# A fused attention and feed-forward kernel on eight cores: one tile's norm per iteration, a pool of eighteen weight buffers, and later quantizing

## What is computed

```python
x = x + layernorm(linear_attn(layernorm(x), W_qkv, W_o))   # 16 heads of 64, chunks, causal, running state S
x = x + layernorm(ffn(layernorm(x)))
# ffn: h = layernorm(x) * gamma + beta
#      h = qlinear(h, w1, b1);  h = gelu(h);  out = qlinear(h, w2, b2)
# qlinear: activations to int8 range by row maximum;
#          weights to -1, 0, 1 by  scale = 1 / mean(|w|);  wq = clip(round(w * scale), -1, 1)
```

## Time and profile before

| what | value |
|---|---|
| median of 3 runs | 1594.47 us (1594.02 to 1597.79) |
| the profiled execution's own time | 1600.33 us |
| its span on the slowest core (core 3) | 1598.8 us |
| spans of the 8 cores | 1577.0 to 1598.8 us |
| PE busy | 1469.1 us, 92% of the span |
| DVE, ACT, POOL busy | 1116.4, 663.3, 277.9 us |

### The profile page before, as it was taken

One profiled execution on the slowest core, in us unless ns is written; L12 is line 12 of the kernel. 1 busy time (PEld: TensorE's weight loads), 2 busy tenths in 40 slices (PEclk: granted clock), 3 DMA queues, 4 the chain that ended last, 5 costly groups with the idle time before them and its releaser, 6 DMA issues.

```text
span 1598.8 us, 26641 instructions; the slowest of 8 cores (1577.0 to 1598.8 us)
## 1 busy us (share of the span) xinstructions
PE 1469.1 (92%) x8948; PEld 727.3 (45%) x8948; DVE 1116.4 (70%) x1861; ACT 663.3 (41%) x1057; POOL 277.9 (17%) x210
## 2 busy tenths in 40 slices
PE   1499589999999999699999999999999999999997
PEld 0255255655555555334444444444444444444443
DVE  6545257676887876677777767777676777767764
ACT  1088478676655555323223232232322323223231
POOL 2011124454676675000000000000000000000000
PEclk9799799999999999899999999999999999999999
DMA  9968957777889985333342533424244242342422
GB/s 226 261 190 241 176 157 217 198 228 219 191 196 200 207 194 160 90 91 78 83 99 61 111 70 81 100 61 114 67 88 94 60 113 69 93 88 60 104 51 66
DMA packets 284005, 209.94 MB, mean 131 GB/s; under 512 B 246616, under 2 KB 246616, under 8 KB 283872
## 3 DMA queue, kind: packets, MB, share of 16 engines
q1 hardware_dynamic: 261776, 131.16, 36.0%
q0 software_dynamic: 22096, 77.08, 17.9%
HBM read 119.03 MB, written 33.55 MB: 95 GB/s over the span
## 4 chain that ended last, share of the span: by engine, by line
PE 63%; DMA 15%; issue 8%; ACT 4%; DVE 3%; DVEq 3%; POOL 2%; ACTq 1%; SPq 0%; POOLq 0%
PE pz L437 28%; PE pp L425 27%; DMA pc<-w 10%; PE pp L315 3%; DMA wost<-w_o 2%; POOL lt L1099 2%; DMA h1f<-h1t 2%; ACT pc L887 1%; PE pp L416 1%; PE pp L333 1%; PE pp L401 1%; DMA kst<-w_qkv 1%; DVEq L723 1%; DVEq L510 1%; DVE wqtp L567 1%
## 5 line engine op out<-in xcount | busy, mean ns | idle before, releaser
L425 PE MATMUL pp<-w1p,xq1f 128*128 128x512 fp8e4 x2048 | 456.5, 381 | 0.0
L437 PE MATMUL pz<-w2p,xq2f 128*128 128x512 fp8e4 x2048 | 447.1, 379 | 0.0
L437 PEld LDWEIGHTS pz<-w2p,xq2f 128*128 128x128 bf16 x2048 | 200.4, 98 | 241.7
L425 PEld LDWEIGHTS pp<-w1p,xq1f 128*128 128x128 bf16 x2048 | 195.8, 98 | 243.5 <-issue 19.2
L636 DVE TENSOR_REDUCE st<-gsb 128x1 f32<-128x1024 f32 x128 | 152.6, 1213 | 130.5 <-ACT gsb L895 130.3
L901 ACT ACT_TABLE_LOAD x31 | 39.8, 1283 | 470.1 <-DVE st L675 470.1
L1099 POOL TENSOR_SCALAR lt<-pc,st 128x1024 bf16<-128x1024 f32 x64 | 188.9, 2952 | 144.5 <-DMA pc<-w 103.7
L895 ACT ACTIVATE gsb<-pp,st 128x1024 f32<-128x1024 f32 x128 | 142.3, 1112 | 102.6 <-PE pp L425 96.8
L315 PE MATMUL pp<-wk,h1f 128*128 128x512 bf16 x512 | 121.9, 391 | 39.2 <-DMA h1f<-h1t 32.4
L315 PE MATMUL pp<-wv,h1f 128*128 128x512 bf16 x512 | 129.7, 399 | 25.3 <-ACT kt L836 14.3
L333 PE MATMUL pp<-h1f,wq 128*128 128x256 bf16 x1024 | 122.6, 280 | 14.0 <-DMA h1f<-h1t 8.9
(11 more groups left out here) (111 smaller groups left out, 1392.2 us busy)
## 6 DMA issues: line engine op xcount, KB each, us to landing
pc<-w POOLq DMA_DIRECT2D x128, 512.0 KB, 6.1
xs<-x SPq DMA_DIRECT2D x32, 512.0 KB, 6.0
x1s<-xs SPq DMA_DIRECT2D x32, 512.0 KB, 4.4
xs<-x1s SPq DMA_DIRECT2D x32, 512.0 KB, 3.4
out<-xs SPq DMA_DIRECT2D x32, 512.0 KB, 3.1
kst<-w_qkv SPq DMA_DIRECT2D x8, 512.0 KB, 12.0
wost<-w_o POOLq DMA_DIRECT2D x8, 512.0 KB, 38.5
wq<-w_qkv POOLq DMA_DIRECT2D x1, 2048.0 KB, 21.4
```

The lines of the kernel that those rows point to most:

```text
L425: mi = PE.matmul(half(n, h), lhsT=xf[:, kk, :], rhs=w1q[:, kk % 4, c0:c0 + 512, kk // 4], start=False, stop=(kk == 7), skip_group_check=True)
L437: mi = PE.matmul(PZ[:, h * 512:(h + 1) * 512], lhsT=xq2f[:, t % 2, kk, :], rhs=w2q[:, kk % 16, h * 512:(h + 1) * 512, kk // 16], start=(kk ...
```

## The change

1. **Norm.** One tile per iteration, three ahead (f = i + 3), in place of two in each even iteration. On DVE `ln1(f)` stands first in the iteration, from i = -1 on. On ACT `ln1_sd(f)` stands right behind `ln2_sd` and `h1(f)` behind `ln3_sd`. On SP `h1_tp(f)` now stands behind the tile load and the first piece's transpose.
2. **Buffers.** All 18 piece buffers form one pool; each load takes the free buffer that was released longest ago, until w1p or w2p covers it. Two loads are in flight, not four. Seven pieces of w1 and five of w2 stay in their buffers from the sum to the quantizing, so that 116 loads remain of 128.
3. **Sums.** 23 of the 64 sums move from ACT to DVE (`piece_vsum`, a reduction of 128 x 1024 float32). Iteration 0 has none. ACT's sums in iterations 1 to 8 are 4, 5, 4, 1, 2, 2, 5, 4, DVE's 2, 1, 1, 5, 3, 4, 1, 1.
4. **Quantizing.** It now runs from iteration 9 to 31: up to 4 pieces in one, 2 in each of the last three. w2 is taken in order of its columns, 0 to 31. PE waits for w2p only ahead of the first `ffn2`.
5. **Layout.** w1p is stored as 32 blocks of 4 x 128, w2p as 8 blocks of 16 x 128, so that a piece's transpose writes one run. The right-hand operand of every `ffn1` and `ffn2` matmul is now four runs of 128 columns, where it was one of 512.
6. **Gamma and beta** are loaded by SP in iteration 30, no longer by POOL.

The diff, cut to its core:

```diff
-    w1p = at("w1p", O_W1, [4, HID], BF16)
+    w1p = at("w1p", O_W1, [NWP, 4, 128], BF16)
...
-    w2p = at("w2p", O_W2, [16, D], BF16)
+    w2p = at("w2p", O_W2, [8, 16, 128], BF16)
...
+    gap, hold = 12, (7, 5)
...
+    bufs = ([pc[:, k] for k in range(2)] + [pc1[:, k] for k in range(8)]
+            + [pc2[:, k] for k in range(8)])
+    covered = ([4 * NWP] * 2 + [place[("quant", 0, 4 * k)] for k in range(8)]
+               + [place[("quant", 1, 4 * k)] for k in range(8)])
+    held = [-1] * 10 + [8] * 8
...
+        z = min((b for b in own if end < covered[b]), key=lambda b: held[b])
...
-                                       rhs=w1q[:, kk % 4, c0:c0 + 512, kk // 4],
+                                       rhs=w1q[:, c0 // 128:c0 // 128 + 4, kk % 4, :, kk // 4],
...
-                                   rhs=w2q[:, kk % 16, h * 512:(h + 1) * 512, kk // 16],
+                                   rhs=w2q[:, 4 * h:4 * h + 4, kk % 16, :, kk // 16],
...
+        def piece_vsum(p):
+            buf, s_ld, landed = piece_buf(p)
+            V.wait_ge(s_ld, landed)
+            V.tensor_reduce(out=c1((acc1, acc2)[p[1]], p[2]), in_=buf, axis=AX.X, op=ALU.add,
+                            apply_absolute_value=True).then_inc(s_vabs, 1)
...
-            t, u, f = i, i + 1, i + 2
-            two = i % 2 == 0 and f < T
-            if two:
+            t, u, f = i, i + 1, i + 3
+            if f < T:
                 ln1(f)
             if 0 <= t - 1 < T:
                 x1(t - 1)
-            if two:
+            if f < T:
                 ln1_r(f)
...
+            if t == T - 2:
+                SP.wait_ge(s_Q, 2 * T)
+                SP.dma_start(out=gam[:], in_=gamma_h.partition_broadcast(128)
+                             ).then_inc(s_gbl[0], 16)
...
+        def load(n):
+            p = loads[n]
+            buf, s_ld, _ = piece_buf(p)
+            if n >= 2:
+                GP.wait_ge(piece_buf(loads[n - 2])[1], piece_buf(loads[n - 2])[2])
+            o, used = prior[p]
+            if not used and where[p][0] >= 10:
+                GP.wait_ge(s_oc, 8)
+            if used and pieces[o][0] == "quant":
+                GP.wait_ge(s_q, nqua[o] + 1)
+            if used and on_dve(pieces[o]):
+                GP.wait_ge(s_vabs, nvsum[o] + 1)
+            if used and pieces[o][0] == "sum" and not on_dve(pieces[o]):
+                GP.wait_ge(s_abs, nsum[o] + 1)
...
+        for q, p in enumerate(pieces):
+            while n < len(loads) and prior[loads[n]][0] <= q - 2:
+                load(n)
+                n += 1
+            if p[0] == "quant":
+                below(p)
```

More of the change, by code:

```diff
@@ new lines, in build @@
+    held = [-1] * 10 + [8] * 8
+    count = [0] * 18
+    loads, where, prior = [], {}, {}
+    for p in pieces:
+        if p[0] == "quant" and p[2] < hold[p[1]]:
+            where[p] = where[("sum", p[1], p[2])]
+            continue
+        stays = p[0] == "sum" and p[2] < hold[p[1]]
+        end = place[("quant", p[1], p[2])] if stays else place[p]
+        own = range(2 + 8 * p[1], 10 + 8 * p[1]) if stays else range(18)
+        z = min((b for b in own if end < covered[b]), key=lambda b: held[b])
+        count[z] += 1
+        where[p] = (z, 16 * count[z])
+        prior[p] = (held[z], count[z] > 1)
+        held[z] = end
+        loads.append(p)
@@ L286, in q_of, with piece_buf, sums_under @@
+    def piece_buf(p):
+        return bufs[where[p][0]], s_pl[where[p][0]], where[p][1]
+    def sums_under(k, z):
+        under = [place[p] for p in pieces
+                 if p[0] == "sum" and not on_dve(p) and where[p][0] == 2 + 8 * k + z // 4]
+        return nsum[max(under)] + 1 if under else 0
     def q_of(t, j):
@@ L493, in pe_program @@
                 ffn1(t + 1, [2, 3])
+            if t == 0:
+                for k in range(4):
+                    PE.wait_ge(s_wtp[k], 16 * 2 * NWP // 4)
             ffn2(t)
@@ L935, in act_program @@
                 q_out(i)
+            if f < T:
+                h1(f)
             if u == T:
                 gelu(0, 1)
-            now = [p for p in plan[t] if p[0] == "sum"] if t >= 0 else []
+            now = [p for p in plan[t] if p[0] == "sum" and not on_dve(p)] if t >= 0 else []
             for p in now[:1]:
```

181 lines of the change are left out of this document (76 added, 105 removed).

## The result

The changed kernel took 1613.97 us (median of 4 runs, 1610.85 to 1616.19), the kernel before, on the same chip, 1595.16 us (4 runs, 1594.02 to 1597.79). The ratio is 1.0109, 95% interval 1.0087 to 1.013 (the two medians by themselves give 1.0118): **the change makes the kernel slower by 1.1%**, where the prediction said 1558 us and faster. All ratios here are over runs in which no die showed a lower granted clock than the other; that leaves out disturbed ones of up to 1722 us.

A forecast was written before the change was run, and what follows sets the result against it. PE's own work bounds the feed-forward part; the attention loop runs 69.8 us over its floor. 1600.3 - 48.8 (loop) + 6.5 (start) + 2 (gamma and beta) = 1560.0, put at 1558 us for the median; range 1545 to 1582 us (0.83).

The forecast's parts named there:

- Sums, 3 us left of 10.7: Iterations 1 to 4: moving sums from ACT to DVE leaves 3 of the 10.7 us over the floor.
- Iteration 5, 5 us left of 21.9: PE's wait for transposes of h1: two loads in flight and spread-out loads leave 5 of 21.9 us.
- The rival of the starved transposes: Iteration 5: loads still hold up h1's transposes, 17 of the 21.9 us more stay, 1575 us; chance 0.09.
- Iterations 6 to 8, 4 left of 8.1: The wait for w1's threshold stays, with one iteration of 5 sums: 4 of 8.1 us over the floor.
- The late loop, 9 us left of 29.1: Iterations 9 to 30: loads issued earlier end the waits for pieces, leaving 9 of 29.1 us over the floor.
- The rival "POOL paces the quantizing": Late loop: POOL, waiting for buffers, paces quantizing as before and the 29.1 us stay, 1578 us; chance 0.08.
- The start, +6.5: Before the first output projection: tile 2's norm in iteration -1 delays tile 0's work, plus 6.5 us, between 3 and 10.
- Tile load, 0: Loop: the norm's tile load lands 0.7 us early enough, costing nothing; rival: late, 1616 us at 2 us, chance 0.09.
- Layout, 0: Feed-forward matmuls: reading four runs of 128 columns costs nothing; rival that they cost: 1583 us, chance 0.04.
- the 25 us of the bound: Layout's upper bound: four runs cost 6 ns more per matmul, 25 us over 4096 matmuls.
- Gamma and beta, +2: End of the loop: loading them in iteration 30 delays `front_a`, plus 2 us, between 0 and 5.
- theory Q: Follow-up theory: POOL's comparisons queue behind unneeded loads; for e1, iteration 9 stays above 25 us, 1600 us or more.

The follow-up runs named there:

- e7: The kernel before with the norm change alone (one tile per iteration, three ahead); ratio 0.9937 to the kernel before.
- e2: The kernel before with two loads in flight instead of four, nothing else changed; ratio 0.9958 to the kernel before.
- e1: The changed kernel with four loads in flight instead of two; ratio 1.0138 to the kernel before.
- e4: The changed kernel with four loads in flight and loads at most eight pieces ahead of the piece under comparison; ratio 1.0085 to the kernel before.
- e14: The changed kernel with loads at most four pieces ahead and three loads in flight instead of two; ratio 0.9948 to the kernel before.
- e16: The changed kernel with DVE's first piece of an iteration, sum or quantizing, behind the masks; 1630.2 us, ratio 1.0199 to the kernel before.
- e13: The changed kernel with loads at most four pieces ahead and DVE's first piece, where it is a sum, behind the masks; ratio 0.9866 to the kernel before.
- e5: The changed kernel with loads at most four pieces ahead of the piece under comparison; ratio 0.983 to the kernel before (two runs).
- e3: The changed kernel with loads at most eight pieces ahead of the piece under comparison; ratio 0.9911 to the kernel before.
- e8: e3 plus a margin: unless due within two pieces, a load waits until its buffer's old piece is four back; ratio 0.9849 to the kernel before.
- e11: The changed kernel with loads at most two pieces ahead of the piece under comparison; ratio 0.9856 to the kernel before.
- e12: The changed kernel with e8's margin for the buffer but no limit on how far ahead a load goes; ratio 0.992 to the kernel before.
- e6: e3 with tile 2's norm in iteration -1 moved behind tile 0's work on DVE and ACT; ratio 0.9902 to the kernel before.
- e10: The kernel before with the norm change and two loads in flight, nothing else; ratio 1.0031 to the kernel before.

## Why the prediction was wrong, point by point

- *Sums, 3 us left of 10.7:* size right. 67.2 - 4 x 16.33 = 1.9 are left, ACT is busy for 53.6 us of them where it was 64.0. But the prediction gave the whole gain to the sums and none to the norm; e7, with the norm change alone, has half of it (75.1 to 71.1, of 67.2).
- *Iteration 5, 5 us left of 21.9:* size right, 0.5 are left. The reason given for it was wrong. The prediction said that the length of the run of loads matters most. e2 keeps the runs and changes only the number in flight, and the stall goes; e1, e4 and e14 bring it back with four or three. The rival of the starved transposes fell for iteration 5: two in flight do not do what four did. What the prediction had no term for is the price of two: the loads come later, and in e2 9.5 of the 17.1 us come back in iteration 7.
- *Iterations 6 to 8, 4 left of 8.1:* wrong, 59.8 - 49.0 = 10.8 are left. The prediction priced the DVE sums at 1.21 us and forgot that one of them stands ahead of the masks and waits there for its piece, 4.1 us on core 1. In e16, the changed kernel with DVE's first piece behind the masks, the median of iteration 7 falls from 23.6 to 18.2; e13 shows the same on e5.
- *The late loop, 9 us left of 29.1:* **this is the step that failed**, by 55 us: 423.2 - 22 x 16.33 = 63.9 are left. "In the late loop a load is issued three to ten pieces ahead of its comparison, so the 103.7 us of waits for pieces should go": most went, down to 21.0 (by the code's order the distance is 0 to 15 pieces). But the prediction costed POOL as work, 3.6 us a piece, and put its waits "for a buffer, for the landing of the load before the last" at nothing beyond the 9 us. The waits in front of loads went from 19.0 to 161.9 us in these iterations, and every comparison queued behind them waits too. e3, e5, e8, e11 and e12 each take 31 to 44 us off the start of the last output projection by an edit of this order alone. The rival "POOL paces the quantizing" named the right engine, with a price of 20 us that had no room for growth: it took the old loss for its upper bound.
- *The start, +6.5:* +5.3 on these cores, +4.9 by the medians. Size right, and ACT waits for the statistics as forecast. The scores start at 88.8 (core 1) where 87.7 was forecast (80.5 + 7.0 is 87.5). Moving the norm in iteration -1 gives back only 1.9 (e6), because there it holds up the second half of Q.
- *Tile load, 0:* right for most iterations. DVE waits for `xs<-x` 6 times, 12.2 us in all, where loads are dense (2.5 us in iteration 9, where PE waits 6.1 for a transpose of h1). It is not what decides here; in e1 it is a large part of iteration 9 (15.0 us). This rival's price at 2 us an iteration, 1616 us, is close to the 1614 measured, by chance: its mechanism is not what the trace shows.
- *Layout, 0:* right. The feed-forward part takes 919.7 us where it took 918.5, with 907.1 us of PE where it was 905.7, and one tile in 28.49 us in both; the 25 us of the bound are excluded.
- *Gamma and beta, +2:* right. The median of iteration 31 grows by 2.8; PE waits 9.7 us for the first quantized tile where it was 7.7.

With the limit of four pieces (e5) the last output projection stands at 639.9, 29.1 us before the 669.0 of the kernel before, where the prediction had 40.3: some seven tenths of the forecast, by an edit of POOL's order alone. One small slip has no part in this: DVE's 13.3 us per iteration less 59 quantizings at 1.28 is 9.8, not 9.6.

What stays open: e5 still has single iterations of 21 to 25 us on single cores (9, 13 and 15 on core 3, for example), and why e10's two waits are longer than e2's.

## What to carry to other kernels

A queue that does loads and work in one order must be costed as a queue: for each piece of work, count what stands ahead of it and what each of those waits for. "The buffer is free, so load early" is right for the buffer and wrong for whatever is queued behind the load; a limit on the distance, here two to eight pieces, was worth 2 to 3%. When a wait is removed by issuing earlier, look for it again at the issue. Don't take the loss of the old kernel as the most that the new one can lose in the same place.

A run that meets a theory's number has not yet met the theory: read in its trace which wait ends last. e1's iteration 9 was long as theory Q said, and for another reason.
